# Gated feed-forward on one Trainium2 core: another order for the last maxima, two activations turned ahead, and VectorE taking three of six product groups

## The reference, cut to what matters

```python
def act_qdq(x):
    qmax = 2.0 ** (ACT_BITS - 1) - 1.0
    scale = jnp.maximum(jnp.max(jnp.abs(x)) / qmax, 1e-12)
    return jnp.clip(jnp.round(x / scale), -qmax - 1.0, qmax) * scale
x = act_qdq(x)
up = act_qdq(x @ lpbq_dequant(w_up).T)
gate = act_qdq(x @ lpbq_dequant(w_gate).T)
sig = fixed_qdq_u16(jax.nn.sigmoid(gate))
gate = act_qdq(gate * sig)
o = act_qdq(gate * up)
return o @ lpbq_dequant(w_down).T
```

## Time and profile before

| What | Value |
|---|---|
| Median of 3 runs | 1427.3 us (1426.59 to 1428.52) |
| Profiled execution, its time | 1428.33 us |
| Its span in the trace | 1426.6 us |
| Mean granted TensorE clock | 0.966 |
| Busy share of the span | PE 93%, DVE 67%, ACT 59%, POOL 30% |
| Gated network in the trace | from 1092.3 us to the end |
| Block of the products, to the last multiply's release of TensorE | 1283.3 to 1327.3 us |

### The profile page before, as it was taken

The page is one execution under the profiler, slowest core; times in us unless marked ns, Lnnn a source line. Parts: engine busy times, 40 slices in busy tenths (PEclk is TensorE's granted clock), DMA queues, the critical chain, the costliest instruction groups (busy, mean ns, idle before and its releaser), DMA issues. The chain is left out here.

```text
span 1426.6 us, 21388 instructions
## 1 busy us (share of the span) xinstructions
PE 1325.1 (93%) x7436; PEld 649.5 (46%) x7436; DVE 953.4 (67%) x1683; ACT 848.7 (59%) x1489; POOL 423.0 (30%) x639
## 2 busy tenths in 40 slices
PE   7999979999999999999999999999998999960798
PEld 4555532333443434434455545554544444420487
DVE  5444428888788887887666688888753335997532
ACT  3545433767777677777755655565563446859432
POOL 0000000024434444345465433333330002549300
PEclk9999986999999999999999999999999999985899
DMA  8677767323242333423323553343110001416132
GB/s 300 230 284 244 270 186 174 101 77 113 61 136 75 108 100 102 136 76 90 114 87 114 153 166 101 99 121 97 58 32 15 0 0 45 171 50 265 46 103 88
DMA packets 87915, 170.75 MB, mean 120 GB/s; under 512 B 14585, under 2 KB 49156, under 8 KB 86276
## 3 DMA queue, kind: packets, MB, share of 16 engines
q1 hardware_dynamic: 87038, 167.70, 36.8%
q10 hardware_dynamic: 774, 1.72, 0.6%
HBM read 108.27 MB, written 60.31 MB: 118 GB/s over the span
## 5 line engine op out<-in xcount | busy, mean ns | idle before, releaser
L1236 DVE TENSOR_REDUCE b_neg_max<-b_score 128x1 f32<-128x512 f32 (+3 forms) x864 | 541.3, 663 | 184.1 <-PE b_score L785 93.5
L1009 ACT ACTIVATE b_probs<-b_exp 128x512 f32<-128x512 f32 (+1 forms) x864 | 463.5, 581 | 282.3 <-PE b_exp L807 281.7
L782 PE MATMUL b_score<-b_k_stack,b_q_stack 97*128 97x512 bf16 (+3 forms) x1024 | 357.1, 352 | 15.3 <-DMA b_k_stack<-s_one 9.4
L807 PE MATMUL b_exp<-b_q_stack,b_k_stack 100*128 100x512 bf16 (+3 forms) x1024 | 345.6, 343 | 6.4 <-ACT b_probs L1009 5.6
L828 PE MATMUL b_av<-b_probs,b_values 128*17 128x512 f32 (+3 forms) x2048 | 229.4, 520 | 3.6 <-POOL b_probs L1107 3.4
L782 PEld LDWEIGHTS b_score<-b_k_stack,b_q_stack 97*128 97x128 bf16 x1024 | 100.0, 98 | 252.3 <-DVE b_neg_max L1236 128.1
L1115 POOL CAST b_max_parts<-b_neg_max 128x16 bf16<-128x16 f32 x64 | 12.8, 201 | 481.5 <-DVE b_neg_max L1236 479.1
L807 PEld LDWEIGHTS b_exp<-b_q_stack,b_k_stack 100*128 100x128 bf16 x1024 | 100.2, 99 | 82.8 <-ACT b_probs L1009 25.0
L1107 POOL TENSOR_SCALAR_AFFINE_SELECT b_probs<-b_probs 128x512 f32<-128x512 f32 x96 | 61.4, 641 | 177.0 <-ACT b_probs L1009 176.5
L785 PE MATMUL b_score<-diag_qk,minus_big 128*128 128x128 bf16 x512 | 113.0, 221 | 0.0
L1663 POOL TENSOR_TENSOR f_hidden<-f_tmp,f_hidden 128x2048 int32<-128x2048 int32 x8 | 44.3, 5531 | 138.4 <-DVE f_tmp L1615 138.4
(11 more groups left out here) (219 smaller groups left out, 1795.8 us busy)
## 6 DMA issues: line engine op xcount, KB each, us to landing
b_q_stack<-s_q SPq DMA_DIRECT2D x384, 64.0 KB
s_k<-a_part_k SPq DMA_DIRECT2D x48, 256.0 KB, 5.7
b_k_stack<-s_k SPq DMA_DIRECT2D x60, 192.0 KB
s_up<-f_up SPq DMA_DIRECT2D x6, 1536.0 KB, 5.1
s_va<-a_va SPq DMA_DIRECT2D x16, 544.0 KB, 5.1
b_values<-s_va SPq DMA_DIRECT2D x16, 544.0 KB, 4.3
a_mask_q<-mask_in SPq DMA_DIRECT2D x8, 1024.0 KB, 7.8
out_dram<-normed SPq DMA_DIRECT2D x16, 512.0 KB, 3.0
```

What stands on the lines that cost most here:

```text
L782: mm = pe.matmul(o, q, KS[half][0:R_MAX, h, 0:w], start=True, stop=causal or not general)
L807: mm = pe.matmul(o, k, QS[half][0:NSTACK, h, q0:T], start=True, stop=not masked)
L1009: nc.scalar.activation(probs[kc][:, h0:h0 + m, q0:T], exp_bank[n % RINGS][:, 0:m * w].rearrange("p (h n) -> p h n", h=m), ACT.Exp).then_in ...
L1236: nc.vector.tensor_reduce(neg_max[u][:, qt, h0:h0 + m], score_bank[n % RINGS][:, 0:m * w].rearrange("p (h n) -> p h n", h=m), AX.X, ALU.ma ...
```

## The change

Three edits, all in `gated_ffn_phase`:

1. In the block of gates and up, VectorE no longer takes the tops of up of batch 6 inside the last step. It takes them after the last `top_pool` and after the gather of act, in two halves around the scale of act, and then all of batch 7.
2. ScalarE turns two batches of act (k = 0 and 1) at the end of that block, not one.
3. In the block of the products ScalarE turns each up batch in two instructions of three groups, groups 3 to 5 first. GpSimd multiplies groups 3 to 5 and waits for the first of the two only. VectorE multiplies groups 0 and 1 as before and, in an instruction of its own, group 2; it waits for both halves.

```diff
+    MINE_OF_PRODUCT = 3
+    AHEAD = 2
...
                     wait_scale(act, "act")
-                    act_to_whole(0)
+                    for k in range(AHEAD):
+                        act_to_whole(k)
...
                         if b > 0:
                             top_pool(b - 1)
-                            top_up(b - 1, 0, FC)
+                            if b < NB - 1:
+                                top_up(b - 1, 0, FC)
...
                     top_pool(NB - 1)
                     gather_on_vector(dve, "act")
-                    top_up(NB - 1, 0, FC - 2)
+                    top_up(NB - 2, 0, FC // 2)
                     scale_on_vector(dve, turn[0], "act")
-                    top_up(NB - 1, FC - 2, FC)
+                    top_up(NB - 2, FC // 2, FC)
+                    top_up(NB - 1, 0, FC)
                     gather_on_vector(dve, "up")
...
-                        sp.wait_ge(prod_by_dve, k - len(ups) + 1)
+                        sp.wait_ge(prod_by_dve, 2 * (k - len(ups) + 1))
...
-                    if k > 0:
+                    if k >= AHEAD:
                         act_to_whole(k)
                     wait_up(act, k)
-                    to_whole(there_whole(k)[:, :, :], there(k)[:, :, :], "up").then_inc(up_by_act, 1)
+                    to_whole(there_whole(k)[:, MINE_OF_PRODUCT:FC, :], there(k)[:, MINE_OF_PRODUCT:FC, :], "up").then_inc(up_by_act, 1)
+                    to_whole(there_whole(k)[:, 0:MINE_OF_PRODUCT, :], there(k)[:, 0:MINE_OF_PRODUCT, :], "up").then_inc(up_by_act, 1)
...
                 def top_pool(k):
                     dve.wait_ge(prod_by_pool, k + 1)
+                    dve.wait_ge(prod_by_dve, 2 * k + 2)
...
-                    dve.wait_ge(up_by_act, k + 1)
+                    dve.wait_ge(up_by_act, 2 * k + 2)
                     nc.vector.tensor_tensor(at(b)[:, 0:MINE, :], whole(b)[:, 0:MINE, :], there_whole(k)[:, 0:MINE, :], ALU.mult).then_inc(prod_by_dve, 1)
-                    dve.wait_ge(prod_by_dve, k + 1)
+                    shared = whole(b)[:, MINE:MINE_OF_PRODUCT, :]
+                    nc.vector.tensor_tensor(shared, shared, there_whole(k)[:, MINE:MINE_OF_PRODUCT, :], ALU.mult).then_inc(prod_by_dve, 1)
+                    dve.wait_ge(prod_by_dve, 2 * k + 1)
...
-                    pool.wait_ge(up_by_act, k + 1)
-                    nc.gpsimd.tensor_tensor(whole(b)[:, MINE:FC, :], whole(b)[:, MINE:FC, :], there_whole(k)[:, MINE:FC, :], ALU.mult).then_inc(prod_by_pool, 1)
+                    pool.wait_ge(up_by_act, 2 * k + 1)
+                    here = whole(b)[:, MINE_OF_PRODUCT:FC, :]
+                    nc.gpsimd.tensor_tensor(here, here, there_whole(k)[:, MINE_OF_PRODUCT:FC, :], ALU.mult).then_inc(prod_by_pool, 1)
...
-                pe.wait_ge(prod_by_dve, NB)
+                pe.wait_ge(prod_by_dve, 2 * NB)
```

## The result

The kernel before took 1427.01 us, median of the 7 runs that stood beside it, and the changed kernel 1432.58 us, median of 7 (1430.87 to 1433.84). The ratio is 1.0039 with a 95% interval of 1.0027 to 1.0050: slower, by 5.6 us, where 6.2 were forecast.

The account below looks back on a forecast made before the run. ScalarE was taken to set the pace of the products, with GpSimd nearly full. VectorE falling a batch behind GpSimd moves the spread from 1334.27 to 1340.5: 1427.3 + 6.2 = 1433.5 us, range for 8 in 10 1427.6 to 1435.2.

Parts of the forecast that it names:

- Tops in another order: End of the gates and up block: scale of act 2.74 us earlier, scale of up and first turn of up 1.05 later.
- the meeting of the engines: Between the scale of up and the first turn of up: expected 1.05 us later, like both of these.
- the interpolation: GpSimd's three-group product, put between 2.13 us for 1024 elements and 4.39 for 2048: 3.3 us.
- Who goes next: In the products, the engine that has waited longer gets in: GpSimd's k = 1 runs before VectorE's second multiply of k = 0.
- The lag: VectorE stays a batch behind in the products, its 0.8 us slack spent waiting; last multiply done at 1334.3, spread 6.2 later.
- The loads of up: In the products, loads from k = 4 on wait for VectorE's later multiplies but still arrive in time: no cost.
- Rival A: VectorE's first multiply in the products is not made to wait for GpSimd: 0.6 us faster, 1426.7; chance 0.13.
- Rival B: In the products VectorE waits at most once per batch and loses no batch: 1.1 us slower, 1428.4; chance 0.16.
- C: GpSimd's three-group product takes 4.2 us of its own, so VectorE loses a second batch: 1439; chance 0.04.
- D: ScalarE's fixed 0.28 us hidden and VectorE never waiting in the products: 3 or 4 us less, 1424; chance 0.03.

Follow-up runs that it names:

- e5: The changed kernel with up turned in one instruction that releases both engines, VectorE still with two multiplies: 1431.32 us.
- e2: The kernel before with edit 3 alone (split turn of up, new shares of the products), tops and act in the old order: 1428.84 us.
- e3: The changed kernel plus one wait: each GpSimd product waits for both VectorE multiplies of the batch before: 1427.11 us.
- e1: The kernel before with edits 1 and 2 alone (tops reordered, two batches of act ahead), products as before: 1425.57 us.
- e4: The changed kernel with VectorE's two multiplies replaced by one-operand reductions of the same length, so three groups go unmultiplied: 1425.42 us.
- e8: e6 plus one wait: each GpSimd product waits for VectorE's multiply of the same batch: 1423.03 us, ratio 0.9965 to the kernel before.
- e6: The changed kernel with VectorE's two multiplies made one of three groups and up turned in one instruction: 1427.12 us.

## Why the prediction was right

Point by point, from the mark's start where a place is meant:
- **Tops in another order.** Scale of act 2.74 earlier expected, 2.74 measured. First turn of up 1.05 later expected, 0.94 measured; the meeting of the engines took 0.1 less.
- **ScalarE.** A batch of 5.86 expected and measured. A turn of 1536 elements has a mean of 1.56, as interpolated.
- **GpSimd.** 3.3 expected for three groups, 3.44 measured where it starts by itself. The 3.3 is what it takes when it has been waiting (4.42 - 1.12 = 3.30): the interpolation used the row of 5.57, in which it was waiting, and so left out 0.13 of starting. Half of that, 0.07, comes through the interpolation; the other 0.1 is open (the row of 2.13 is a float32 instruction). It moved the ends that VectorE waits for by 0.1 and adds up nowhere, since each product starts with ScalarE's turn and not with the product before. The sentence beside it, with the estimate of 3.4 from the Trainium skill's page "GPSIMD Engine Reference", section 3.1, was the nearer one.
- **Who goes next.** The step on which the forecast hung, taken from one place with instructions of 0.4 and 0.7 us, held for one of 3.4: the second multiply took 3.92. It rested on thin evidence: in rows 10 and 11 VectorE's instructions are TENSOR_SCALAR with one tensor as operand (`b_mv` and `b_rstd` give one number per partition), and the forecast read them as if they were multiplies with two. e5 shows the step again without the split, e2 and e3 that it vanishes when GpSimd isn't waiting yet. e1 shows the other direction: there GpSimd's products follow each other without a gap, and VectorE, which waits, gets in between. So it is the engine that waits which goes next, and not GpSimd always.
- **The lag.** VectorE's slack of 0.8 a batch went into waiting: the multiply takes 2.00 to 2.03 in steady state, 0.8 over 1.21. Its last multiply ended 69.72 after the mark's start, where 1334.3 - 1264.57 = 69.7 was forecast. The spread moved by 6.15 where the forecast had 6.2, and the medians by 5.6 (3.9 to 7.1 by the interval).
- **The loads of up** came at no cost, as said: no row of ScalarE in the products waits for one.
- **Rival A** (no wait) fell: not one of VectorE's multiplies of 1024 elements inside a product of GpSimd took 1.23. e4 shows what A would have given. **Rival B** (no lost batch) fell for this kernel, and e3 shows that its size was right. **C** and **D** fell with the 3.44 and the 2.0.

The Trainium skill's rule (page "SBUF — State Buffer", section "Who interferes with whom"), that a VectorE instruction with two SBUF inputs and a GpSimd instruction that reads SBUF exclude each other and the second is held until the first is done, is now borne out for long waits as well: at k = 0 VectorE waited 1.9 us (3.09 against 1.23) and then 3.2 (3.92 against 0.68). At 1206.41 VectorE's one-operand L1615 was held too, while e4's reductions were not: one operand less does not lift the wait by itself.

What I had not seen is that the loss was not in the change's plan but in its form. Three groups for each engine, act ahead and the tops reordered make a faster kernel, as e8 shows, once VectorE's share is one instruction and the order is fixed. Whether the one instruction is needed when the order is fixed isn't shown: e3 keeps two and won back 4.9, but its wait fixes another order.

Left open: why the start of the mark varies by 3 us between executions of the same code. And e8 has one turn of up where the change has two; a kernel with VectorE first and the turn split was not tried, nor one with VectorE first and two multiplies.

## What to carry to other kernels

Where VectorE instructions with two SBUF operands and GpSimd instructions work side by side, count them as one engine: add their times per batch, give each side one instruction per batch, and fix who goes first with a semaphore, even though it is one wait more. An instruction that is split in two lets the other engine in between if that engine is already waiting, and the second part then pays for a whole product. Then ask which engine ends last: in e8 the pair is faster than ScalarE, and ScalarE sets the time. A busy share says nothing about this: compare an instruction's length with that of the same form elsewhere in the trace.

## What the runs showed of the hardware that I had not expected

- The order of the two engines can be decided by 0.08 us and then stay: e6 lost 3.3 us of mark against its forecast by one late start, and one wait (e8) gave it back.
- The parts of a change need not add up: -0.45 and +2.8 made +6.15, because one part brought about the meeting that made the other costly.
- TensorE's granted clock stays at 0.50, the level of 1.2 GHz, all through the products and rises again within the 16 matmuls, but not at a fixed point. Before, it was 0.50 over their first 5.36 us; in the changed kernel it was still 0.50 over the first 5.21 us. In e8, where they start at 1323.75, it had a mean of 0.56 over the first 2.75 us and was 1.00, the level of 2.4 GHz, over the next 0.5, and the window around them (columns as above) has a mean of 0.74:
```profile
1322.50:1329.50 7.00, 5.14 (x18) 2.24 (x20) 6.16 (x6) 0.00 (x0) 3.43 (x1) 0.74 0.00 0
```
  Where the 16 matmuls decide it, the spread came 5.66 (e6), 5.74 (e5), 5.78 (e3) and 6.07 us (the change) after their start. Where VectorE's tops decide it, as in e8, the clock's rise does not move it.
